# Global attention, then two local streams, against three streams in one written order (one core)

## The chip, the cores and the metric

The kernel runs on one core of one Trainium2 chip. TensorE (PE, with its weight loads as PEld), VectorE (DVE), ScalarE (ACT), GpSimd (POOL) and SyncE (SP, which issues DMAs here) each run their own list of instructions in order, and wait for one another on semaphores. The metric is the device time of one execution in microseconds, lower is better.

## The reference, cut to what matters

```python
x = L0_attn_x                                     # (8, 512, 128)
mod = (_silu(c) @ wmod).reshape(8, 6, 1, 128)     # sa, ca, ga, sb, cb, gb; |ga|, |gb| at least 0.25
h = _layernorm(x) * (1 + ca) + sa
x = x + ga * attn(h)                              # 16 heads of 8, softmax over all 512
h = _layernorm(x) * (1 + cb) + sb
x = x + gb * ffn(h)                               # two layers of the local transformer

def attn(x):          # global attention
    q, k, v = (x @ W + b).reshape(b, 16, 8, 512)
    a = softmax(einsum('bhdt,bhds->bhts', k, v) * temperature)
    return einsum('bhdt,bhts->bhds', q, a)

def layer(x, ...):    # local attention, 8 heads of 64, windows of 64
    q, k, v = split(shift_token(x) @ wqkv)
    q, k = rotary_xpos(l2norm(q) * qs, l2norm(k) * ks)
    x = x + local_attention(q, k, v) @ wo         # each window sees itself and the one before
    h = layernorm(shift_token(x)) * lg + lb
    a, g = split(h @ w1 + b1)
    return x + (a * gelu(g)) @ w2 + b2
```

All 8 batch elements ("batches" below) are independent of each other. A batch's local layers need that batch's global attention to be done.

## The kernel before

**Two phases.** The first does the global attention of all 8 batches (functions `a_...`), the second both local layers of all 8 (functions `b_...`). Every engine waits between them until the last batch of the first phase is added to `x_sb` (`a_over`).

**Phase A.** A batch takes 32 steps. In a step `a_scores` makes two 128x512 tiles of scores into one of three PSUM slots of two banks (L1072), `a_max` takes their row maxima on DVE (L828), `a_exp` makes the exponentials and their sums on ACT (L544) into `E`, a ring of four. Two steps make a group: `a_sums` inverts the sums (L832), POOL scales the queries by them (L455), and `a_values` multiplies them into `O_BANK` (L1082, 32 columns of the array for each of four heads). The scores have a contraction of 32 (four products of high and low parts by a head of 8). `k_rows` holds each head's 32 rows among 96 rows of zeros, so that one product over all 128 rows gives the head's scores; POOL zeroes it at the start (L446). Beside the steps stands the preparation of the next batch (layer norm, transpose, projections, `a_split`), at fixed steps. Batches 1 to 6 run in a register loop.

**Phase B.** Two streams, x for the even batches and y for the odd ones, four each, write their steps as generators; `merge` interleaves them by one string of x and y per engine (`ORDER`). Each stream has its own buffers and four PSUM banks, used in rotation (`b_take`). A layer is: projections by `i` (q, k, v of a quarter of the tokens, L1120), squares on ACT (L575), rotation on DVE (L859, L863) and sums of squares (L867), `b_norm` over q and k of all tokens (L872) with a Newton step (L784 to L786), the scaling on POOL (L472), transposes (L1127), then 8 heads of scores (L1136 with the mask, L1143), maxima (L884), exponentials (L603), scaling (L477), transposes (L1153) and values (L1164), then the output projection (L1174), layer norm and the gated hidden layer (L1193, L915, L1199). Exponentials and GELU need different tables of ACT.

**Ahead of phase A** DVE makes the gates of all batches as 128x2048 rows (`gates`, L752 to L759) and the rotary tables (`tables`, L766 and L770).

Of the kernel before, what the change touches and what calls it, by code (L numbers as in the profile page):

```python
# [14 lines left out]
P = 128  # L15
# [3 lines left out]
HQ = 4  # L19
# [15 lines left out]

GROUPS = [(hh, j) for hh in range(HQ) for j in range(J)]
NG = len(GROUPS)
STEPS = 2 * NG
SLOTS = 3
SLOT_USES = [len(range(k, STEPS, SLOTS)) for k in range(SLOTS)]  # L40
E_RING = 4
# [4 lines left out]
PREP = ["xT", "qT", "k", "v"]  # L46
PREP_AT = {"var": 1, "rsqrt": 2, "normal": 4, "xT": 6, "hT": 8, "qT": 9, "queries": 11, "k": 11, "v": 15}
SPLIT_AT = {"k": 13, "v": 17}


STREAMS = 2
B_BANKS = 4
# [4 lines left out]
PT_SLOTS = 4  # L57
LN_CHAIN = 2 + 3
B_CHAIN = LN_CHAIN + (2 + LN_CHAIN) * L


def bank_uses():
    out = [("x2T",)]
    for l in range(L):
        for i in range(J):
            out += [("q", l, i), ("k", l, i), ("v", l, i)]
        for i in range(J):
            out += [("qT", l, i), ("kT", l, i)]
        for n in range(NU + AV_LAG):
            if n < NU and n % 2 == 0:  # L70
                out += [("sim", l, n), ("sim", l, n + 1)]
            if 0 <= n - PT_LAG < NU:
                out.append(("pT", l, n - PT_LAG))
            if n >= AV_LAG and (n - AV_LAG) % 2:
                out.append(("av", l, (n - AV_LAG) // 2))
        out += [("wo", l), ("tok", l), ("lnT", l)]
        out += [(name, l, c) for name in ("gate", "up") for c in range(3)] + [("w2", l)]
    return out + [("yT",)]


B_USES = bank_uses()
B_USE = {s: i for i, s in enumerate(B_USES)}
B_PER = [len(range(k, len(B_USES), B_BANKS)) for k in range(B_BANKS)]

# [4 lines left out]
        "xxxxxxxxxxxxxxxxyxxyxyxxyxxyyyyxxyxxxyxyyxxxyxxxxxyxyyyxyyyyyxyxxxxxxyxyyxxxyyxxxxxyyyxyxxxyyyyyyxxy"  # L89
        "xxxxxxyxxyyyxyyyxyxxxyxyyyyyyxxxyyyxyxxxyxxyyxyyyyxyyxxxxyyxxxyyxyyyyxyyyxxxxxyyxxyxxxxyxyyxyxxxxyxy"  # L90
        "xyyyyyxyxyxxxxyxxyyyyyyyyxxyyxxyyxxxxxxyyxyyyyyyxyxxxxyyxxxyyyyxyxxxyxyxxxyxxxyyxyyyyxxyxxxxxyxyyyyy"
        "yxyxxyyxyyxxxyxyyxyxxyyyxxyxxxxyyxyyyyyxyxxxxxxyxyxyyyxyyxxxxxxyyyyxxxxyxyxyyyyxxyxxxxxyxyyyyyyxyxyx"
        "xxyxxyyxyyyyyxxxyyxyyyxxxxxyyxyyyyyyxyxxxyyxxxxyyxxyyxyxxyyxxyxxxxxyyyyyyxxyxxxxxxyxyyyyxxyyyxxyyyxx"
        "yyyyxxxxyyxyyxxxyxxyyxyyyyxyxyxyxxxxyxyyxyyyyxyyyxxxxxyyxxxxxxyyxyyxyxxxxyxyyyyyyxyxyxxyxxyyyyxxxyyy"
        "xyxxyxyxyyxxxxxyyxyyyyyyxyxxxxyyxxxyyxyyxxxxxxyyyyxxyxxyxyyyyxxyxxxxxyxyyyyyyxyxxyyyyyxyxxxyyyxxxxyx"
        "yyxxxxyxyyxyyyyyyyxyyxyyyxyxxyyxxyyxyyyxyyyyyyyyyyyy"
    ),
    "DVE": (
        "xxxxxxxxxxxxxyyyyxyxxxxxxxyyxxyxxxyyxxxxxyxyyxxxxxxyyyyyyyxxxyxxyyxxyyyxxxyyxyyyxyxxyxyyyyyxxxxxxxyy"
        "yxyyxxxxxyyyyxxyxxxyxyyyxyxxxxxyxyyxxyyyyxyxxyyxyyyyyxyyyxxxxxyxxxyxyxyyyyyyyxyxxyxxyxxxyxxyxxxyyyyy"  # L100
        "xxyxxxyxyyxyxxxxxyyyyxyxxyyyxxyyyyyxxxxyxyyyyxyxxxyxyyyyyxyyyxxxyyxxxxyxxyxxyxyxyxxxxyxyyyxyxxxxxyxx"
        "xyyyxyyxxyxyyyxyyyxxxxyyyyyxxyxxyxxyyyyyxyyyxxxyxyyxxyxxxyxxxyyyyxxyxxyxxyyyxyxxxxxyyyyyxxyyxyxxyyxy"
        "yyxxxyyxyyyxxyxxyxyyyyyxxxxyxyyxxxyyxxyyxxxyyxxyxxxyxyyyxxyxxxxyyyxxxyyyyyxxxyyxyyyyxyyyyxyxxxxxxyxx"
        "yxyyyyyyyyxyyxxyxxxxyxyyxxyxxxyyxxyxxxyxyyxyxxxxxyyyyxyxyxyyxxyyxyyyxxxyyxyyyxyxxxyxyyyyyxyyyxxxyyxx"
        "xxyyyxxyxxxyxxyxxxyxyyxyxxxxxyyyyyyyyyyyyyyyxxxyyyyxyxyyyyyyyyyy"
    ),
    "ACT": (
# [20 lines left out]
def merge(streams, order):  # L128
    for c in order:
        next(streams["xy".index(c)])  # L130
# [1210 lines left out]
```

## Time and profile before

| what | us |
|---|---|
| median of 3 runs | 1343.25 (1342.24 to 1343.5) |
| the profiled execution's own time | 1344.58 |
| its span, first to last instruction | 1342.2 |
| PE busy | 1093.8 |
| DVE busy | 978.8 |
| ACT busy | 912.8 |
| POOL busy | 466.6 |

The profiled execution lies 1.3 us over the median. No engine is busy for the whole span, so the question at every place is which engine is nearest to full there and what holds it up. Busy time of PE is modelled at its ends and its matmuls overlap, so it is read as a load with some air in it.

### The profile page before, as it was taken

What the parts mean: (1) busy time and instruction counts of PE and PEld (TensorE: products, weight loads), DVE (VectorE), ACT (ScalarE), POOL (GpSimd) and SP (SyncE); (2) the same over time, 40 slices, a digit from 0 to 9 for tenths busy, and PEclk for the clock granted to TensorE, in tenths of its full rate; (3) what the DMA queues carried; (4) which work ended last, traced back from release to release, by engine and by line L of the source; (5) the groups of instructions that cost most, each with busy time, mean ns of one, the idle gap of its engine ahead of it and who ended that gap; (6) DMA issues with size and microseconds to landing.
All of it is one profiled execution on the core that took longest, in us unless ns stands there. A gap on an engine that the chain in (4) does not pass through costs nothing. (4 is left out here: it accounts for less than half of the span.)

```text
span 1342.2 us, 24422 instructions
## 1 busy us (share of the span) xinstructions
PE 1093.8 (81%) x8120; PEld 569.9 (42%) x8120; DVE 978.8 (73%) x1937; ACT 912.8 (68%) x2746; POOL 466.6 (35%) x524
## 2 busy tenths in 40 slices
PE   4588888888888668988878789787888887888886
PEld 3233233233232235555545555454544454454553
DVE  5989888988988777668567586575775766856843
ACT  1588897898888736766646667566576574766662
POOL 2000000000000057357254464362653634545630
PEclk9699998999999979999888999888999998899988
DMA  5442241340331001110101101101001010111010
GB/s 182 161 126 64 64 126 32 94 118 25 109 103 23 0 0 30 29 29 1 37 0 37 28 2 29 36 1 36 9 21 29 1 37 0 37 29 29 1 29 16
DMA packets 24546, 59.04 MB, mean 44 GB/s; under 512 B 2736, under 2 KB 2928, under 8 KB 23280
## 3 DMA queue, kind: packets, MB, share of 16 engines
q1 hardware_dynamic: 24432, 57.62, 15.2%
q8 instruction: 59, 0.97, 0.3%
q14 instruction: 55, 0.45, 0.1%
HBM read 23.98 MB, written 18.87 MB: 32 GB/s over the span
## 5 line engine op out<-in xcount | busy, mean ns | idle before, releaser
L544 ACT ACTIVATE E<-slot,neg_max 128x512 f32<-128x512 f32 x512 | 344.2, 731 | 76.8 <-DVE neg_max L828 68.8
L828 DVE TENSOR_REDUCE neg_max<-slot 128x2 f32<-128x1024 f32 x256 | 306.0, 1212 | 39.6 <-PE slot L1072 39.5
L1072 PE MATMUL slot<-v_rows,k_rows 128*128 128x512 f32 x512 | 214.1, 489 | 61.1 <-ACT E L544 50.5
L477 POOL TENSOR_TENSOR rot_work<-rot_work,rz 128x512 f32<-128x512 f32 x128 | 133.2, 1042 | 325.0 <-DVE rz L889 324.9
L603 ACT ACTIVATE rot_work<-bank,neg 128x128 f32<-128x128 f32 x512 | 181.2, 376 | 64.6 <-DVE neg L884 41.6
L1072 PEld LDWEIGHTS slot<-v_rows,k_rows 128*128 128x128 f32 x512 | 92.1, 197 | 245.4 <-ACT E L544 213.2
L1120 PE MATMUL bank<-wqkv_sb,hs 128*128 128x512 f32 x384 | 188.2, 617 | 8.3 <-DVE rot_work L863 4.8
L463 POOL TENSOR_TENSOR work<-work,rot_work 128x512 f32<-128x512 f32 x128 | 162.9, 1273 | 78.3 <-DVE rot_work L863 74.4
L455 POOL TENSOR_TENSOR qz<-qT,rz 128x32 f32<-128x32 f32 x128 | 30.7, 240 | 416.9 <-DVE rz L832 416.9
L1082 PE MATMUL o_bank<-E,qz 128*32 128x512 f32 x1024 | 143.6, 635 | 1.7 <-POOL qz L455 1.7
L472 POOL TENSOR_TENSOR work<-work,rn 128x512 f32<-128x512 f32 x128 | 131.2, 1061 | 23.4 <-DVE rn L786 23.4
L544 ACT ACTIVATION_READ_ACCUMULATOR E<-slot,neg_max 128x1 f32 x512 | 127.5, 249 | 0.0
L884 DVE TENSOR_REDUCE neg<-bank 128x4 f32<-128x512 f32 x128 | 85.6, 679 | 45.1 <-PE bank L1143 44.7
L603 ACT ACTIVATION_READ_ACCUMULATOR rot_work<-bank,neg 128x1 f32 x512 | 109.9, 215 | 0.0
L1193 PE MATMUL bank<-work,w_sb 128*128 128x512 f32 (+1 forms) x192 | 104.4, 687 | 4.9 <-ACT work L618 2.7
L1153 PE MATMUL bank<-ident,rot_work 128*128 128x128 f32 x512 | 84.5, 292 | 25.7 <-POOL rot_work L477 13.6
L859 DVE TENSOR_TENSOR work<-bank,rot 128x512 f32<-128x512 f32 x128 | 86.7, 677 | 19.4 <-ACT rot_work L575 19.2
L575 ACT ACTIVATE rot_work<-bank 128x512 f32<-128x512 f32 x128 | 76.8, 613 | 34.9 <-PE bank L1120 20.1
L1120 PEld LDWEIGHTS bank<-wqkv_sb,hs 128*128 128x128 f32 x384 | 67.0, 193 | 75.9 <-issue 49.7
L1153 PEld LDWEIGHTS bank<-ident,rot_work 128*128 128x128 f32 x512 | 60.7, 147 | 70.7 <-POOL rot_work L477 45.2
L863 DVE TENSOR_TENSOR rot_work<-bank,rot 128x512 f32<-128x512 f32 x128 | 86.9, 679 | 0.0
L867 DVE TENSOR_REDUCE ss<-rot_work 128x8 f32<-128x512 f32 x128 | 86.3, 675 | 0.0
(120 smaller groups left out, 1652.4 us busy)
## 6 DMA issues: line engine op xcount, KB each, us to landing
v_rows<-v_scr SPq DMA_DIRECT2D x8, 1024.0 KB, 6.4
k_rows<-k_scr SPq DMA_DIRECT2D x32, 256.0 KB, 7.4
work<-v_al SPq DMA_DIRECT2D x16, 512.0 KB, 4.4
work<-v_al SPq DMA_DIRECT2D x16, 384.0 KB, 6.6
k_scr<-hi SPq DMA_DIRECT2D x16, 256.0 KB, 3.0
k_scr<-lo SPq DMA_DIRECT2D x16, 256.0 KB, 3.2
v_scr<-hi SPq DMA_DIRECT2D x16, 256.0 KB, 3.1
v_scr<-lo SPq DMA_DIRECT2D x16, 256.0 KB, 3.5
```

What stands on the lines that cost most here:

```text
L463: pool.tensor_tensor(qk[s][:, i, w, :], qk[s][:, i, w, :], sinp[s][:, n % 2, :], ALU.add).then_inc(rot_sum[s], 1)
L472: pool.tensor_tensor(v, v, rn[s][:, i, w, :].unsqueeze(2).broadcast_to([P, H, DH]), ALU.mult).then_inc(qk_ready[s], 1)
L477: pool.tensor_tensor(pr[s][:, u % PR_SLOTS], pr[s][:, u % PR_SLOTS], rz2[s][:, u, :].unsqueeze(2).broadcast_to([P, 4, 2 * W]), ALU.mult).t ...
L544: act.activation(E[:, g % E_RING, 2 * half + m, :], slot[:, m], ACT.Exp, bias=neg_max[:, n, m:m + 1], accum_out=z[:, n, m:m + 1]).then_inc ...
L603: last = act.activation(pr[s][:, u % PR_SLOTS, w, :], bank[:, 2 * W * w:2 * W * (w + 1)], ACT.Exp, bias=neg2[s][:, u, w:w + 1], accum_out= ...
L828: dve.tensor_reduce(neg_max[:, n, :], slot[:], AX.X, ALU.max, negate=True).then_inc(max_ready, 1)
L863: dve.tensor_tensor(sinp[s][:, n % 2, :].rearrange("p (h a r) -> p h a r", h=H, a=2), bank[:].rearrange("p (h a r) -> p h a r", h=H, a=2)[ ...
L1072: last = pe.matmul(bank, k_rows[:, hh, q, P * j:P * (j + 1)], v_rows[:, par, q, :], start=True, stop=True)
L1082: last = pe.matmul(O_BANK[32 * q:32 * q + 32, :], qz[:, hh, j % QZ_SLOTS, q, :], E[:, g % E_RING, q, :], start=(g == 0), stop=(g == NG - 1))
L1120: pe.matmul(bank[:], hs[s][:, P * i:P * (i + 1)], wqkv_sb[:, l, INNER * c:INNER * (c + 1)], start=True, stop=True).then_inc(full, 1)
L1153: last = pe.transpose(bank[:, P * w:P * (w + 1)], pr[s][:, u % PR_SLOTS, w, :], ident[:])
L1193: pe.matmul(bank[0:CH[c]], w1_sb[:, l, o:o + CH[c]], h2T[s], start=True, stop=True).then_inc(full, 1)
```

## The change

**Streams.** There are three generators now: `a` for global attention, `x` and `y` for the local layers. `ORDER` interleaves all three on all five engines. x takes batches 0, 1, 2, 4, 6 and begins as soon as batch 0 has left global attention; y takes 3, 5, 7 and begins when `a` is through (`enter_wait`), in the SBUF that `a` leaves. There are no register loops any more.

**Scores.** `k_rows` and `v_rows` hold 32 rows for each head, laid out so that the four heads of a group lie in different row quarters. Each score product is 32 rows by 128 columns, and the two of a step stand in neighbouring quarters. The zeroed rows and their memset are gone. Loads of `v_rows` and `k_rows` are seven DMAs each.

**Buffers.** One pool of eight PSUM banks; `BANKS` says which bank every use takes, bank 7 being `O_BANK` until `a` is over. `E` is a ring of three (four before), `kf` single (double before), `prT` two slots (four before).

**Local layers.** Projections of k and v come first, then those of q; the norm is in two halves (k, then q), each with its own `b_norm`, `b_rnorm` and pair of ACT instructions; `b_norm` takes its factor from a tensor `clamp`.

**Start.** The gates are worked out on 128x16 columns and spread by PE (16 products) and ACT (4 copies); the rotary tables are made on POOL; the first batch's `v` goes over ACT's DMA queue; the loads of `x` for batches 1 to 7 stand behind the first batch's parts.

```diff
-E_RING = 4
+E_RING = 3
...
-PT_SLOTS = 4
+PT_SLOTS = 2
...
+BATCHES = [[0, 1, 2, 4, 6], [3, 5, 7]]
+ROTATIONS = [(i, w) for w in (1, 0) for i in range(J)]
...
 ORDER = {
     "PE": (
-        "xxxxxxxxxxxxxxxxyxxyxyxxyxxyyyyxxyxxxyxyyxxxyxxxxxyxyyyxyyyyyxyxxxxxxyxyyxxxyyxxxxxyyyxyxxxyyyyyyxxy"
+        "aaaaaaaaaaaaaaaaaaaaaaaaaaaaaaaaaaaaaaaaaaaaaaaaaaaaaaaaaaxaxxxxxxxxxaaaaxxaaaaxaaaaxxxaaaaaxxxaaaaa"
...
+        def enter_wait(eng, s, k):
+            if s and k == 0:
+                a_over(eng)
...
-                for m in range(2):
-                    q = 2 * half + m
-                    bank = a_take(pe, b, n, m)
-                    last = pe.matmul(bank, k_rows[:, hh, q, P * j:P * (j + 1)], v_rows[:, par, q, :],
-                                     start=True, stop=True)
-                last.then_inc(a_full[n % SLOTS], 1)
+                pair = take_pair(pe, [("a", b, "s", n, m) for m in range(2)])
+                for m, (bank, full) in enumerate(pair):
+                    r = 32 * ((2 * half + m + hh) % HQ)
+                    pe.matmul(bank, k_rows[r:r + 32, hh, P * j:P * (j + 1)], v_rows[r:r + 32, b % 2, hh, :],
+                              start=True, stop=True).then_inc(full, 1)
...
-            pool.memset(k_rows[:].bitcast(F32), 0.0).then_inc(k_zero, 1)
+            pool.memset(qz[:], 0.0).then_inc(s_qz, 1)
+            pool.memset(clamp[:], SHIFT2).then_inc(s_clamp, 1)
...
-                dve.tensor_scalar(ss[s][:], ss[s][:], NORM_MIN2, SHIFT2, ALU.max, ALU.mult).then_inc(ss_all[s], 1)
+                v = ss[s][:, :, w, :]
+                dve.scalar_tensor_tensor(v, v, NORM_MIN2, clamp[:], ALU.max, ALU.mult).then_inc(ss_all[s], 1)
...
-            merge(streams, ORDER["DVE"])
+            merge([a_stream(), b_stream(0), b_stream(1)], ORDER["DVE"])
```

DVE at the start, before. `slot` and `gate_bc` hold the gates, `rot` the rotary tables; the last row is the first step's maxima.

```order
L822 TENSOR_TENSOR lo<-kf,hi 128x512
L752 COPY gate_bc<-slot 128x2x256 x4
L756 TENSOR_SCALAR E<-gate_bc 128x2048
L757 SCALAR_TENSOR_TENSOR E<-gate_bc 128x2048
L758 TENSOR_SCALAR E<-E 128x2048
L759 SCALAR_TENSOR_TENSOR gate_bc<-E 128x2048
L766 TENSOR_TENSOR rot<-rot,rows 128x4x64
L770 TENSOR_TENSOR rot<-rot,rows 128x4x32 x2
...
L828 TENSOR_REDUCE neg_max<-slot 128x2 x2
```

The same place now:

```order
L1131 TENSOR_TENSOR lo<-kf,hi 128x512
L1073 SCALAR_TENSOR_TENSOR gate_col<-gate_col 128x16
L1074 TENSOR_SCALAR gate_col<-gate_col 128x16
L1075 TENSOR_SCALAR gate_col<-gate_col 128x16
L1076 SCALAR_TENSOR_TENSOR gate_col<-gate_col 128x16
L1137 TENSOR_REDUCE neg_max<-psum 128x2 x2
```

Four short rows stand between the first split and the first maxima; the tables are on POOL.

DVE in global attention, before (the batch ahead of the register loop): maxima (`neg_max`), sums, and the preparation of the next batch, and nothing else.

```order
L828 TENSOR_REDUCE neg_max<-slot 128x2 x2
L832 RECIPROCAL rz<-z 128x4
L828 TENSOR_REDUCE neg_max<-slot 128x2 x2
L832 RECIPROCAL rz<-z 128x4
L815 SCALAR_TENSOR_TENSOR kf<-prep_bank,cols,rows 128x512
L820 CAST hi<-kf 128x512
```

DVE in the third batch of `a` now, with stream x's first layer (`work`, `rot_work`, `ss`, `nt`, `rn`) in between:

```order
L1210 TENSOR_REDUCE ss<-rot_work 128x8
L1216 SCALAR_TENSOR_TENSOR ss<-ss,clamp 128x4x8
L1137 TENSOR_REDUCE neg_max<-psum 128x2 x2
L1202 TENSOR_TENSOR work<-psum,rot 128x512
L1206 TENSOR_TENSOR rot_work<-psum,rot 128x512
L1210 TENSOR_REDUCE ss<-rot_work 128x8
L1141 RECIPROCAL rz<-z 128x4
L1137 TENSOR_REDUCE neg_max<-psum 128x2 x2
L1089 SCALAR_TENSOR_TENSOR nt<-ss,rn 128x4x8
```

The half norm over k stands in the middle of the rotations, and steps of `a` stand between x's.

PE in global attention, before: products of scores (`slot`) and of values (`o_bank`) by turns.

```order
L1072 MATMUL slot<-v_rows,k_rows 128x512 x4
L1082 MATMUL o_bank<-E,qz 32x512 x4
L1072 MATMUL slot<-v_rows,k_rows 128x512 x4
L1082 MATMUL o_bank<-E,qz 32x512 x4
L1072 MATMUL slot<-v_rows,k_rows 128x512 x2
```

PE where stream x begins now:

```order
L477 MATMUL psum<-ident,rot_work 128x128 x4
L429 MATMUL psum<-v_rows,k_rows 128x512 x2
L484 MATMUL psum<-wqkv_sb,hs 128x512 x9
L429 MATMUL psum<-v_rows,k_rows 128x512 x2
L405 MATMUL psum<-ident,xn 128x128 x4
L438 MATMUL psum<-E,qz 32x512 x4
L429 MATMUL psum<-v_rows,k_rows 128x512 x2
L484 MATMUL psum<-wqkv_sb,hs 128x512 x2
```

x's transposes and projections (nine in a row at one place) stand between the score products of `a`, so full-array products and 32-row products take turns.

## Rows read from the trace of the kernel before

**Rows 1.** The page's head and section 1: busy time of each engine.

```profile
span 1342.2 us, 24422 instructions
...
PE 1093.8 (81%) x8120; PEld 569.9 (42%) x8120; DVE 978.8 (73%) x1937; ACT 912.8 (68%) x2746; POOL 466.6 (35%) x524
```

**Rows 2.** Section 2 of the page: busy tenths in 40 slices.

```profile
PE   4588888888888668988878789787888887888886
...
DVE  5989888988988777668567586575775766856843
ACT  1588897898888736766646667566576574766662
```

**Rows 3.** Three lines: minimum/median/maximum ns, then first and last start, us.

```profile
L828 DVE TENSOR_REDUCE neg_max<-slot x256: 1189/1215/1226, 46.3 to 455.1; 128x2 f32<-128x1024 f32 x128
...
L840 DVE TENSOR_TENSOR x_sb<-x_sb,o_gated x8: 691/693/693, 103.9 to 460.7; 128x512 f32 x6, 128x512 f32<-128x512 f32 x2
...
L1072 PE MATMUL slot<-v_rows,k_rows x512: 387/496/796, 41.3 to 454.7; 128*128 128x512 f32 x171
```

**Rows 4.** Stretches: us, then PE, PEld, DVE, ACT, POOL busy, granted clock, DMA share, GB/s.

```profile
45.00:470.00 425.00, 357.71 (x1689) 130.62 (x1690) 368.25 (x587) 363.09 (x1056) 30.71 (x128) 0.94 0.25 76
500.00:1300.00 800.00, 671.25 (x6116) 400.83 (x6115) 542.16 (x1218) 518.20 (x1626) 404.09 (x365) 0.94 0.09 22
```

**Rows 5.** Section 5 of the page: busy us, mean ns | idle before, releaser.

```profile
L544 ACT ACTIVATE E<-slot,neg_max 128x512 f32<-128x512 f32 x512 | 344.2, 731 | 76.8 <-DVE neg_max L828 68.8
L828 DVE TENSOR_REDUCE neg_max<-slot 128x2 f32<-128x1024 f32 x256 | 306.0, 1212 | 39.6 <-PE slot L1072 39.5
L1072 PE MATMUL slot<-v_rows,k_rows 128*128 128x512 f32 x512 | 214.1, 489 | 61.1 <-ACT E L544 50.5
...
L1082 PE MATMUL o_bank<-E,qz 128*32 128x512 f32 x1024 | 143.6, 635 | 1.7 <-POOL qz L455 1.7
```

**Rows 6.** Waits in 500 to 1300 us: us in total, times, longest.

```profile
PE bank L1136 <- ACT rot_work L603: 17.5, 16, 3.6
...
PEld bank L1120 <- DVE rot_work L863: 15.9, 21, 1.6
...
PEld bank L1127 <- POOL work L472: 14.5, 24, 1.6
```

**Rows 7.** Timeline of DVE over 0 to 60 us: start us, us, instruction.

```profile
4.96 6.29 DVE L734 TENSOR_SCALAR cT<-cT 128x8 f32<-128x8 f32 x1 [0.33 <-ACT cT L516]
...
31.65 2.87 DVE L752 COPY gate_bc<-slot 128x512 f32<-128x512 f32 x4 [3.63 <-PE slot L1039]
...
46.28 2.35 DVE L828 TENSOR_REDUCE neg_max<-slot 128x2 f32<-128x1024 f32 x2
...
49.94 0.17 DVE L781 TENSOR_SCALAR var_e<-mv 128x4 f32<-128x4 f32 x1
```

**Rows 8.** Timeline of POOL over the same stretch.

```profile
4.30 6.92 POOL L446 MEMSET k_rows<- 128x8192 f32 x1
```

**Rows 9.** Timeline of PE at the start, and in three short windows of global attention.

```profile
41.34 2.90 PE L1072 MATMUL slot<-v_rows,k_rows 128*128 128x512 f32 x6 [9.73 <-issue]
...
205.27 0.63 PE L1072 MATMUL slot<-v_rows,k_rows 128*128 128x512 f32 x2
...
210.33 0.50 PE L1072 MATMUL slot<-v_rows,k_rows 128*128 128x512 f32 x1 [0.17 <-ACT E L544]
210.76 0.95 PE L1082 MATMUL o_bank<-E,qz 128*32 128x512 f32 x4
```

**Rows 10.** Section 6 of the page, a DMA issue: KB each, us to landing.

```profile
v_rows<-v_scr SPq DMA_DIRECT2D x8, 1024.0 KB, 6.4
```

**Rows 11.** DVE's groups by form, 500 to 1300 us: busy us, mean ns.

```profile
L872 DVE TENSOR_SCALAR ss<-ss 128x64 f32<-128x64 f32 x15 | 12.2, 811 | 0.4
...
L781 DVE TENSOR_SCALAR var<-mv 128x4 f32<-128x4 f32 x21 | 7.6, 362 | 0.7
...
L784 DVE SCALAR_TENSOR_TENSOR nt<-ss,rn 128x64 f32<-128x64 f32 x15 | 3.6, 237 | 1.4 <-ACT rn L585 1.2
```

More of the change, by code:

```diff
@@ L321, in b_see, with place, empty @@
-        def b_see(eng, s, k, step):
-            m, n = b_at(step)
-            eng.wait_ge(b_full[s][m], k * B_PER[m] + n + 1)
-            return banks[B_BANKS * s + m], b_free[s][m]
-        def b_done(eng, s, k, *steps):
+        bank_of = iter(BANKS)
+        places, used = {}, [0] * 8
+        def place(m, step):
+            places[step] = (m, used[m])
+            used[m] += 1
+            return psum[:, m], full[m]
+        def empty(pe, m):
+            if used[m]:
+                pe.wait_ge(free[m], used[m])
+            elif m == 7:
+                a_over(pe)
@@ new lines, in take, with take_pair, see @@
+        def take(pe, step, *read):
+            m = int(next(bank_of))
+            empty(pe, m)
+            done(pe, *read)
+            return place(m, step)
+        def take_pair(pe, steps, *read):
+            m = int(next(bank_of))
+            empty(pe, m)
+            empty(pe, m + 1)
+            done(pe, *read)
+            return place(m, steps[0]), place(m + 1, steps[1])
+        def see(eng, step):
+            m, n = places[step]
+            eng.wait_ge(full[m], n + 1)
+            return psum[:, m], free[m]
@@ L327, in b_done, with see_pair, done @@
+        def see_pair(eng, first, second):
+            m, _ = places[first]
+            see(eng, second)
+            return psum[:, m:m + 2], (free[m], free[m + 1])
+        def done(eng, *steps):
             need = {}
             for step in steps:
-                m, n = b_at(step)
+                m, n = places[step]
                 need[m] = max(need.get(m, 0), n + 1)
             for m, n in need.items():
-                passed(eng, b_free[s][m], k * B_PER[m] + n)
+                eng.wait_ge(free[m], n)
@@ L334, in stand, with b_take, b_see, b_done @@
+        def b_take(pe, s, k, step, *read):
+            return take(pe, (s, k) + step, *((s, k) + r for r in read))
+        def b_see(eng, s, k, step):
+            return see(eng, (s, k) + step)
+        def b_done(eng, s, k, *steps):
+            done(eng, *((s, k) + step for step in steps))
         def stand(eng):
@@ new lines, in gate_rows @@
+            def gate_rows():
+                pe.wait_ge(s_gcol, 1)
+                for g in range(2):
+                    for n in range(2):
+                        bank, full = take(pe, ("gate", g, n))
+                        for i in range(4):
+                            c = g * B + 4 * n + i
+                            last = pe.matmul(bank[:, D * i:D * (i + 1)], gate_col[:, 0, c:c + 1].broadcast_to([D, P]),
+                                             ident[:], start=True, stop=True)
+                        last.then_inc(full, 1)
@@ L1053, in a_project_q @@
-                pe.matmul(bank[:], wq_sb, hT[:].rearrange("p j n -> p (j n)"), start=True, stop=True).then_inc(p_full, 1)
+                bank, full = take(pe, ("a", b, "qT"), ("a", b, "xT"))
+                pe.matmul(bank, wq_sb, hT[:].rearrange("p j n -> p (j n)"), start=True, stop=True).then_inc(full, 1)
             def a_project(b, step):
                 w = wk_sb if step == "k" else wv_sb
-                bank = p_take(pe, b, step)
+                bank, full = take(pe, ("a", b, step))
```

1583 lines of the change are left out of this document (801 added, 782 removed).

## The prediction

> **What bounds the kernel now.** I read the page's head first, then the slices, then stretches, then the groups. The head says that no engine is full: PE is busy 1093.8 us of 1342.2, DVE 978.8, ACT 912.8 [rows 1]. So the order of the work costs time, and a merge can give back at most the difference between 1342 and about 1094. The slices show two regimes [rows 2]: up to slice 13 all three engines stand at 8 or 9, afterwards PE stands at 7 to 9 and DVE and ACT at 5 to 7.
>
> The border is in the source rows: global attention runs from the first maxima at 46.3 us to the last residual, which ends at 461.4 [rows 3]. That is 415.1 us, 51.9 for a batch. The local layers take the 880.8 us that are left, 110.1 for a batch with two streams side by side.
>
> The stretches give the loads [rows 4]. In global attention, over 425 us: DVE 368.25, ACT 363.09, PE 357.71, so 46.0, 45.4 and 44.7 us per batch; the fullest engine, DVE, reaches 0.866. POOL is nearly idle there (30.71). In the local layers, over 800 us (7.27 batches at 110.1): PE 671.25, DVE 542.16, ACT 518.20, POOL 404.09, so 92.4, 74.6, 71.3 and 55.6 us per batch; the fullest, PE, reaches 0.839. Global attention is thus bound by DVE and ACT, the local layers by PE, and the two are never beside each other: the change puts them there.
>
> **The score products.** Today 512 products occupy PE for 214.1 us, 0.42 each [rows 5]. Two of them back to back cover 0.63 us [rows 9], and the shortest record of one is 387 ns [rows 3], so the pitch is about 0.24. The values' products show what quarters of the array do: 1024 of 635 ns, a sum of 650 us, in 143.6 us of busy time [rows 5]; four run at once, since 4 of them cover 0.95 us [rows 9]. If row quarters do the same, a pair takes one pitch fewer. The saving lies between 0 and 214.1/2 = 107 us of PE time, 0 to 13.4 per batch. I take 10, since the pairs also have latency that stays. PE was not the fullest engine in that phase, so alone this gives no time; it makes room for stream x: PE 34.7 per batch of `a`.
>
> Against that stands the change of the array's form. Inside one form the pitch is 0.24, and from a score product at 210.33 to the values' at 210.76 it is 0.43 [rows 9], up to 0.2 us for one change of form. Stream x's full-array products now come between 32-row products, so I add one or two changes to each of some 220 steps: 220 x 0.1 to 220 x 0.4, 22 to 88 us of PE; I take 40. The Trainium skill (TensorEngine Tiling (Array Packing), Key Properties) says the same, that changing the tiling mode drains the engine while changing only the tile does not; it gives no figure. By that rule the larger end would hold, PE would have 48 us more than I take, and the sum below would grow only if PE became the bound.
>
> **The start.** Today the first score product runs at 41.34 after 9.73 us of idle PE [rows 9], which is the wait for the loads of `v_rows` and `k_rows` (`v_rows` needs 6.4 us to landing [rows 10]); the first maxima come only at 46.28, because gates and tables hold DVE from 31.65 [rows 7]. The change takes those 14.6 us off DVE; by themselves they hide the loads, so just 46.28 - 41.34 = 4.9 us of them count. DVE's first small instruction also took 6.29 us, and it ended as POOL's memset of `k_rows` ended, at 11.2 [rows 7, 8]; others of its size take 0.2. Without that memset the chain may start up to 6 us earlier. The Trainium skill (SBUF — State Buffer, SBUF: two separate sides) describes DVE and GpSimd sharing a port pair under an exclusive lock, which is what these two rows look like. Against it: 14 loads instead of 5 behind one another, some of 3 us of issue, and ACT issues `v`'s DMAs in front of its gate copies and first exponentials. So the first maxima come at 35 to 44; I take 38.
>
> **Phase 1, `a` beside x.** The order table says how far things get. x's first step on DVE stands behind 1.12 batches of `a`, and ahead of the last step of `a` stand 204 steps of x of 87 per batch, 2.34 batches (PE's table gives 2.32). The first 1.13 batches run as today: 1.13 x 51.9 = 59 us. It remains 6.87 batches of `a` and 2.33 of x:
> DVE: 6.87 x 46.0 + 2.33 x 75 = 491; ACT: 6.87 x 45.4 + 2.33 x 72 = 480 (0.7 a batch for its new pair of instructions in each layer); PE: 6.87 x 34.7 + 2.33 x 92.4 + 40 = 494; POOL 26 + 130 = 156.
> The norm in halves costs DVE a second clamp and three more Newton instructions: 3 x 0.24 = 0.7 us a layer; `b_norm` itself, 811 ns for 64 columns, is dear today [rows 11] and may cost 0.3 to 0.8 each. That is -0.2 to +1.5 us a layer, and I have put 0.4 a batch. POOL beside `a` also hurts DVE's short instructions: L781 takes 362 ns in the local layers [rows 11] and 0.17 us where POOL is idle [rows 7]. About 13 such a batch at half of 0.19, since POOL is half as busy here, are 8 us in all. DVE: 499.
> What share of the time can it be busy? 0.866 was reached with one stream, 0.839 by PE with two. Here three engines are near equal, which leaves no slack, but each wait of `a` can now be filled by x. Lower bound 0.80, upper 0.95; I take 0.89, a little over `a` alone: 499/0.89 = 561. Phase 1 ends at 38 + 59 + 561 = 658.
>
> What is queued behind the new waits: `a_exp` of group g now waits for the values of group g-3 (a ring of three), and those wait on PE for POOL's scaling, in front of which x's 1.0 to 1.3 us steps stand in POOL's list. While PE waits there, x's products wait too. I count nothing for it beyond the 0.89, since the sums are ready about two steps ahead.
>
> **Phase 2, x beside y.** It remains 8 - 2.33 = 5.67 batches; at today's pace 5.67 x 110.1 = 624 us. About 8 us of that go, since today both streams enter empty (slice 14 shows PE at 6 [rows 2]) and now x is in the middle of a layer. The pool of banks and the early k half can take away at most the waits of PE for banks and for POOL's scaled tiles: (15.9 + 17.5 + 14.5)/7.27 = 6.6 us a batch [rows 6], 37 us in all; the two slots of `prT` work against it, since the ACT copy of the next pair now waits for the values of the last one. From -10 to 37; I take 16. Phase 2: 600 us.
>
> **Sum.** 658 + 600 = 1258, and 2.4 us outside the span (1344.58 - 1342.2): 1260 us, 6.2% below the median. Of the 83 us, phase 1 carries all: 2.33 batches of local layers have cost 257 us and now cost 658 - 461 = 197.
>
> **Rivals.**
> 1. *Near-full merge.* DVE at 0.95 in phase 1 (525 us), first maxima at 35, and phase 2 takes the bank waits and more (575): 35 + 59 + 525 + 575 + 2 = 1196. For it: two independent streams seldom wait at once, and the whole order is written out. Against: neither phase of before came over 0.87. Chance 0.15.
> 2. *y's chain paces phase 2.* y must do three batches after `a`. A stream of before needs 880.8/4 = 220 us a batch; 3 x 220 = 660 instead of 600, so 1320. For it: steps within a layer depend on each other, and y cannot start earlier. Against: the tables let y go ahead (x has done 2.6 of its last batches when y is at 2.9). Partly so: 1280 to 1320. Chance 0.17.
> 3. *Row quarters don't overlap, and forms drain dearly.* PE in phase 1 then has 494 + 69 + 48 = 611, and at 0.93 it needs 657 instead of 561: 1356 at the worst, about 1300 if only one of the two holds. Against: the column quarters overlap fully [rows 5, 9]. Chance 0.08.
> 4. *Slower.* The ring of three and POOL's order stop PE, and PE's list stops x as well. DVE's share in phase 1 decides: with phase 2 at 624, the total reaches 1343 when the stretch takes 620 us, a share of 0.80. On a share of 0.84, 20 of the 110 groups held up 1.3 us each are enough for that; at 0.76 the time is 1380. Today such waits of PE are 1.7 us in all [rows 5], with POOL idle. Chance 0.06.
> That `a` and x don't in fact overlap is no rival here: the order rows show them interleaved.
>
> **Chances and range.** The forecast (1225 to 1280) has 0.54. The range 1195 to 1330 takes in the near-full merge and y's chain, and leaves out rival 4, the worst of 3 and what lies below 1195, together under 0.2. A difference of 0.2% is about what a measurement of this kernel can tell from no change. Faster by more: 0.93; within: 0.01; slower: 0.06.
>
> **What would show it.** First maxima at 38 (35 to 44). The last residual of `a` at 658; DVE's share between x's start and there 0.89. Score products in pairs, both starting within some 20 ns, with a total busy time near half of 214 us. Phase 2 of 600 us with PE at 0.87 or more. If PE waits for `qz` for more than 20 us in phase 1, rival 4 is at work; if PE stands under 0.8 in phase 2 while y never waits for x, rival 2. The forecast is wrong in its core if phase 1 takes over 740 us or DVE's share there is under 0.8.

## The result and the profile after

| | before | after |
|---|---|---|
| median, us | 1343.38 (1342.24 to 1346.27) | 1305.48 (1304.58 to 1308.16) |
| span of the profiled execution, us | 1342.2 [rows 1] | 1303.6 |
| granted clock, mean | 0.935 | 0.895 |
| end of global attention, us | 461.4 [rows 3] | 707.3 |

The ratio is 0.9718, with a 95% interval of 0.9697 to 0.9739: 37.9 us less. The forecast was 1260, 83 us less. The direction was right and the time lies inside the range, but under half of the gain arrived. In the experiments below a ratio leaves out executions that took over 1.5% longer than the fastest of the same kernel.

The page of after, its head, three of its slice lines and four groups (columns as in [rows 1, 2, 5]):

```profile
span 1303.6 us, 23771 instructions
...
PE 1065.7 (82%) x8124; PEld 530.6 (41%) x8124; DVE 976.1 (75%) x1985; ACT 923.0 (71%) x2782; POOL 466.8 (36%) x537
...
PE   4078878988878789878888889898888988888987
...
DVE  3096988897788789787996875876795688677755
...
PEclk8575889988888999698788999989999989999999
...
L843 ACT ACTIVATE E<-psum,neg_max 128x512 f32<-128x512 f32 x512 | 348.3, 714 | 100.0 <-DVE neg_max L1137 77.5
L1137 DVE TENSOR_REDUCE neg_max<-psum 128x2 f32<-128x1024 f32 x256 | 306.9, 1213 | 86.4 <-PE psum L429 85.3
...
L429 PE MATMUL psum<-v_rows,k_rows 32*128 32x512 f32 x512 | 137.2, 556 | 99.6 <-ACT E L843 45.8
```

The slices show two things. The second one, 33 to 65 us, is all but empty: PE, which began with 4 and 5 before [rows 2], has 4 and 0. And from there PE stands mostly at 8 and 9, in the first half together with DVE. The idle time of DVE before its maxima has grown from 39.6 us [rows 5] to 86.4; one wait at the start makes 42.7 us of it.

The phases are read off three lines of after: the score maxima, the last residual of global attention, and `kT`'s memset, the first instruction on DVE that belongs to one local stream alone (first x, then y). Minimum/median/maximum ns, then first and last start:

```profile
L1137 DVE TENSOR_REDUCE neg_max<-psum x256: 1153/1216/1226, 63.5 to 693.9; 128x2 f32<-128x1024 f32 x128
...
L1152 DVE TENSOR_TENSOR x_sb<-x_sb,kf x8: 691/692/1040, 128.5 to 706.6; 128x512 f32<-128x512 f32 x8
...
L1279 DVE MEMSET kT<- x2: 272/272/272, 129.2 to 709.0; 128x256 f32 x2
```

| term | forecast | after | error |
|---|---|---|---|
| first maxima | 38 | 63.5 | +25.5 |
| `a` alone, 1.13 batches | 59 | 65.7 | +6.7 |
| `a` beside x | 561 | 578.1 | +17.1 |
| x beside y | 600 | 596.3 | -3.7 |
| span | 1258 | 1303.6 | +45.6 |

More than half of the error is there before the first maximum is taken. The timeline of after, PE and then ACT's and SP's queues (start us, us, instruction, idle before it; ACTq and SPq issue DMAs):

```profile
20.79 6.10 PE L397 MATMUL psum<-ident,gate_col 128*128 128x128 f32 x32 [4.38 <-DVE gate_col L1076]
62.60 1.22 PE L429 MATMUL psum<-v_rows,k_rows 32*128 32x512 f32 x6 [35.71 <-DMA v_rows<-v_scr]
...
26.93 13.64 ACTq L857 DMA_DIRECT2D v_rows<-v_scr  x7
...
24.81 7.41 SPq L655 DMA_DIRECT2D k_rows<-k_scr  x7
32.27 14.26 SPq L639 DMA_DIRECT2D x_sb<-in_x  x7
```

PE had done everything else by 26.9 us and stood 35.71 us for `v_rows`. Before, PE was idle for 9.73 us at this place [rows 9; the row names no releaser], and the megabyte needed 6.4 us to landing [rows 10]. Now the issue alone takes 13.64 us, and the last part lands at about 62.

Three stretches of after (us, then PE, PEld, DVE, ACT, POOL busy with counts, granted clock, DMA share, GB/s): `a` alone, `a` beside x, x beside y:

```profile
63.50:128.00 64.50, 50.36 (x222) 14.83 (x220) 50.90 (x87) 50.59 (x147) 4.09 (x17) 0.63 0.21 70
128.00:707.00 579.00, 484.58 (x3333) 204.74 (x3333) 485.84 (x888) 473.79 (x1422) 157.54 (x229) 0.89 0.17 54
707.00:1300.00 593.00, 515.40 (x4508) 297.88 (x4503) 428.36 (x975) 392.83 (x1206) 294.80 (x267) 0.95 0.08 21
```

The middle one is the merge: DVE 0.839, PE 0.837, ACT 0.818 of the time. The last has PE at 0.869, against 0.839 in the local layers before [rows 4]. The clock is new: 0.63 while `a` runs alone, where global attention had 0.94 before [rows 4].

### The profile page after: what moved, and what is told of

Read it like the earlier page. It is cut to its first block and busy times, and to the rows that moved or that the text cites. A ratio compares the mean times of both kernels' runs of the same rounds, so it can differ in the third digit from the quotient of the medians.

```text
span 1303.6 us, 23771 instructions
## 1 busy us (share of the span) xinstructions
PE 1065.7 (82%) x8124; PEld 530.6 (41%) x8124; DVE 976.1 (75%) x1985; ACT 923.0 (71%) x2782; POOL 466.8 (36%) x537
## 5 line engine op out<-in xcount | busy, mean ns | idle before, releaser
L843 ACT ACTIVATE E<-psum,neg_max 128x512 f32<-128x512 f32 x512 | 348.3, 714 | 100.0 <-DVE neg_max L1137 77.5
L1137 DVE TENSOR_REDUCE neg_max<-psum 128x2 f32<-128x1024 f32 x256 | 306.9, 1213 | 86.4 <-PE psum L429 85.3
L429 PE MATMUL psum<-v_rows,k_rows 32*128 32x512 f32 x512 | 137.2, 556 | 99.6 <-ACT E L843 45.8
L484 PE MATMUL psum<-wqkv_sb,hs 128*128 128x512 f32 x384 | 195.7, 636 | 11.5 <-DVE rot_work L1206 3.8
L939 ACT ACTIVATE rot_work<-psum,neg 128x128 f32<-128x128 f32 x512 | 184.3, 407 | 26.4 <-DVE neg L1228 18.5
L438 PE MATMUL psum<-E,qz 128*32 128x512 f32 x1024 | 164.2, 718 | 0.0
L939 ACT ACTIVATION_READ_ACCUMULATOR rot_work<-psum,neg 128x1 f32 x512 | 124.8, 247 | 0.0
L843 ACT ACTIVATION_READ_ACCUMULATOR E<-psum,neg_max 128x1 f32 x512 | 118.6, 232 | 0.0
L491 PE MATMUL psum<-ident,work 128*128 128x128 f32 x512 | 89.2, 312 | 29.4 <-POOL work L784 14.0
L559 PE MATMUL psum<-work,w_sb 128*128 128x512 f32 (+1 forms) x192 | 99.4, 645 | 6.7 <-ACT work L954 4.3
```

The source lines that it names most:

```text
L429: pe.matmul(bank, k_rows[r:r + 32, hh, P * j:P * (j + 1)], v_rows[r:r + 32, b % 2, hh, :], start=True, stop=True).then_inc(full, 1)
L438: last = pe.matmul(O_BANK[32 * q:32 * q + 32, :], qz[:, hh, j % QZ_SLOTS, q, :], E[:, (b * NG + g) % E_RING, q, :], start=(g == 0), stop=( ...
L484: pe.matmul(bank, hs[s][:, P * i:P * (i + 1)], wqkv_sb[:, l, INNER * c:INNER * (c + 1)], start=True, stop=True).then_inc(full, 1)
L491: last = pe.transpose(bank[:, P * p:P * (p + 1)], qk[s][:, i, w, P * p:P * (p + 1)], ident[:])
L559: pe.matmul(bank[0:CH[c]], w1_sb[:, l, o:o + CH[c]], h2T[s], start=True, stop=True).then_inc(full, 1)
L843: act.activation(E[:, (b * NG + g) % E_RING, 2 * half + m, :], pair[:, m], ACT.Exp, bias=neg_max[:, n, m:m + 1], accum_out=z[:, n, m:m + 1 ...
```

## Experiments

The ratios below are to the kernel before, run on the same chip; its medians there lie between 1343.2 and 1346.8.

### One DMA for each head's 32 rows

**Theory A**: the new loads are slow because of their shape. The view of the source for two to four heads is `"q t d s -> q (t d) s"`, with the heads outermost, a dimension of 2, 3 or 4, where before it was 128 rows for `v_rows` (`"q h t d s -> (h t d) q s"`) and 32 for each part of `k_rows`. **Theory B**: the number of DMAs and their issue are the cost; more of them are slower still. The edit gives each head its own DMA (16 instead of 7 for each of `k_rows` and `v_rows`), whose outermost dimension is the 32 rows.

```diff
-K_LOADS = [1, 2, 2, 2]
+K_LOADS = [4, 4, 4, 4]
...
-                for q in ((0, HQ),) if hh == 0 else ((0, HQ - hh), (HQ - hh, HQ)):
-                    r = 32 * ((q[0] + hh) % HQ)
-                    sp.dma_start(dst[r:r + 32 * (q[1] - q[0])].bitcast(F32),
-                                 scr[q[0]:q[1], hh].rearrange("q t d s -> q (t d) s")).then_inc(landed, 16)
+                for q in range(HQ):
+                    r = 32 * ((q + hh) % HQ)
+                    sp.dma_start(dst[r:r + 32].bitcast(F32),
+                                 scr[q, hh].rearrange("t d s -> (t d) s")).then_inc(landed, 16)
```

> The changed kernel with each load of k_rows and v_rows cut into single heads of 32 rows (64 KB), 16 DMAs instead of 7, the same bytes to the same places. Theory A (shape of the loads): a DMA whose outermost dimension on the DRAM side counts 2, 3 or 4 heads is moved by only 2, 3 or 4 of the 16 DMA engines, and that is what holds the first score product until 62.6 us; with 32 rows outermost all 16 work, v_rows lands some 7 us after its last issue, the first maxima come at 38 to 43 instead of 63.5, and the 4.9 us wait at the first border of batches goes too: 1305.5 - 25 = about 1280, 1276 to 1286. Theory B (volume or queue): the loads are slow because the x and weight loads run beside them, or because ACT's queue is slow; more and smaller DMAs then change nothing or cost issue time: 1303 to 1312 and first maxima at 60 or later.

Measured: 1268.31 us (1262.82 to 1270.2), ratio 0.9425 (0.9379 to 0.9471). Its span was 1266.2, 37.4 less than after's. PE and the queues at its start:

```profile
39.38 1.22 PE L429 MATMUL psum<-v_rows,k_rows 32*128 32x512 f32 x6 [12.58 <-DMA v_rows<-v_scr]
...
26.85 7.50 ACTq L857 DMA_DIRECT2D v_rows<-v_scr  x16
...
25.03 7.45 SPq L655 DMA_DIRECT2D k_rows<-k_scr  x16
32.52 3.46 SPq L639 DMA_DIRECT2D x_sb<-in_x  x7
```

Sixteen DMAs take 7.50 us to issue where seven took 13.64 (on SP, `k_rows` takes 7.45 where it took 7.41), and the wait falls from 35.71 to 12.58 us. So Theory A, with 12 us more of gain than it had expected; the next experiment looks for them. How many engines move the data is shown by the DMA view over the stretch in which `v_rows` is on its way, first after from 29 to 62 us, then this kernel from 26 to 40 (busy tenths of the core's 16 DMA engines in 40 slices; then ACT's queue, q10, with packets, MB and share of 16 engines):

```profile
DMA  2523222211669841297886897899998999994111
...
q10 hardware_dynamic: 557, 1.05, 9.6%
```

```profile
DMA  6548587838886999997999977899999969999999
...
q10 hardware_dynamic: 793, 1.08, 30.2%
```

The same megabyte is spread over 33 us at 9.6% of 16 engines (16 x 0.096, one and a half at work), or goes through in 14 us at 30.2% (nearly five, with the keys' loads and weights on the rest). The Trainium skill (DMA: Bandwidth & Descriptors, Why a DMA increments its semaphore by 16 and not by 1) has the rule: a DMA runs on as many engines, 16 at most, as divide the slowest dimension of both sides. By it a source with 2, 3 or 4 heads outermost gets at most that many and one with 32 rows gets 16. Both traces agree with that, though they show shares of a stretch and not the engines of one DMA. This edit changes the number of DMAs together with their shape; that the number isn't what helps is seen in the kernel before, where a single DMA with 128 rows outermost brought the same megabyte in 6.4 us [rows 10].

### The loads of the first batch alone

Is it the start alone, or every border of batches? Only batch 0's loads are split by head; the later ones keep their shape.

```diff
+                if first:
+                    for q in range(HQ):
+                        ...
+                    return
...
-                a_rows(k_rows[:, hh], k_scr, hh, k_in[hh])
+                a_rows(k_rows[:, hh], k_scr, hh, k_in[hh], b == 0)
```

> The changed kernel with per-head loads for the first batch alone; the loads of the seven batches after it keep the changed kernel's shape. It splits the 37 us that per-head loads gave (1305.5 to 1268.3). Theory A: the first batch's loads, which nothing hides, are 23 us of it (first maxima at 40.2 instead of 63.5), and the later loads the other 14, by waits at the batches' borders and by SP's queue: 1282, 1278 to 1286, and the 4.9 us wait for k_rows at the first border comes back. Theory B: the later loads are hidden, and the 14 us came from elsewhere (order of arrival after an earlier start): 1268 to 1273.

Measured: 1279.36 us (1276.66 to 1280.72), ratio 0.9508 (0.9461 to 0.9555). The maxima start at 40.3, as with all loads split (40.2), but `a` ends later. `kT`'s memset, that is x's start and y's, in this kernel:

```profile
L1293 DVE MEMSET kT<- x2: 272/272/272, 105.7 to 684.8; 128x256 f32 x2
```

With all loads split the two stand at 101.0 and 671.5: x starts 4.7 us later here, and the stretch from there to y takes 579.1 us instead of 570.5. So Theory A: about 26 us of the 37 belong to the first batch's loads and about 11 to the later ones, though those have a whole batch of time to land. In after the only visible trace of them is a wait of 4.9 us for `k_rows` at the first border; the rest I have not placed.

### What 32-row products do by themselves

**Theory A**: the new form of the product is good for the first phase or neutral, since PE isn't its fullest engine. **Theory B**: it has a price of its own, which the merge hides. The kernel before, with products over the 32 rows in which a head's data stand (same values, same order; both products of a step in one row quarter):

```diff
+                    r = slice(32 * hh, 32 * hh + 32)
-                    last = pe.matmul(bank, k_rows[:, hh, q, P * j:P * (j + 1)], v_rows[:, par, q, :],
+                    last = pe.matmul(bank, k_rows[r, hh, q, P * j:P * (j + 1)], v_rows[r, par, q, :],
```

> The kernel before with only the form of the score products changed: 32 rows (the head's own) instead of 128 rows of which 96 are zeros. Both products of a step lie in the same row quarter, so they can't run at once; layout, loads and order are as before. Theory A (32-row products lower the granted clock): in global attention the clock falls from 0.95 to 0.8 or less, as in the changed kernel's first batch (0.63), and a batch takes 54 to 57 us instead of 51.9: 1343 + 16 to 40 = 1360 to 1383. Theory B (the clock was low in the changed kernel only because PE had stood idle for 36 us and x had not begun): the clock stays at 0.93 to 0.95 and the time within 4 us of 1343.

Measured: 1454.72 us (1451.42 to 1459.26), ratio 1.0823 (1.0772 to 1.0874): 110 us slower through this edit alone. Global attention, and the local layers behind it:

```profile
45.00:575.00 530.00, 512.54 (x1684) 179.01 (x1684) 365.42 (x562) 368.43 (x1052) 30.79 (x128) 0.55 0.20 61
600.00:1400.00 800.00, 662.84 (x6052) 397.05 (x6052) 550.20 (x1235) 515.32 (x1606) 410.43 (x372) 0.94 0.09 22
```

To be set beside [rows 4]: DVE and ACT have the same work (365.42 and 368.43 us against 368.25 and 363.09), PE has 512.54 instead of 357.71 with the same count, and the granted clock is 0.55 instead of 0.94, that is, the array was at the lower of its two levels (1.2 GHz) for most of the phase. The local layers are untouched. PE had become the bound. Is the reason its clock, or the form itself, with its changes between score and value products? Three stretches of this phase in the same trace, at three mean clocks, answer (the first two are short, half a batch each):

```profile
120.00:145.00 25.00, 22.36 (x110) 8.79 (x106) 21.53 (x31) 20.12 (x57) 1.68 (x7) 0.86 0.16 47
195.00:220.00 25.00, 23.42 (x105) 8.72 (x107) 20.62 (x30) 20.55 (x61) 1.69 (x7) 0.77 0.56 158
245.00:570.00 325.00, 321.14 (x1006) 112.40 (x1006) 213.02 (x311) 219.45 (x624) 18.28 (x76) 0.50 0.17 52
```

At a clock of 0.86 DVE is busy for 0.861 of the time (21.53 of 25), as in the kernel before (0.866); at 0.77 for 0.825; at 0.50, the lower level throughout, for 0.655. PE runs 3.1 products per us there, against 4.4 in the first stretch. So most of the loss goes with the clock; why the clock stays low is not shown. The loss was far more than either expectation held.

### One after the other

Does the merge pay, then? Loads split by head, and the order table of the three streams rewritten, and with it the bank table `BANKS`: first all of `a`, then x's part of 2.33 batches alone, then x beside y as in after.

```diff
 ORDER = {
     "PE": (
-        "aaaa...aaxaxxxxxxxxxaaaaxxaaaaxaaaa..."
+        "aaaa...aaaaaaaaaaaa...xxxxxxxxxxxx..."
```

> Per-head loads, and the order tables changed so that all of a's steps come first and then x's steps that stood between them (2.33 batches); what follows is the same. Nothing overlaps in phase 1. It shows what a costs alone in its new form and what x costs alone. Theory A (phase 1 is short of engine time, DVE above all): a alone takes 52 to 56 us a batch, 415 to 450 in all, x alone 2.33 batches of 150 to 190 us (it is bound by the chain of its own steps), 350 to 440; phase 1 then takes 770 to 890 and the run 1400 to 1530. Theory B (a in its new form is itself slow, which eats the overlap): a alone takes over 480 us.

Measured: 1573.05 us in one run, span 1571.2. `a` alone and x alone:

```profile
41.00:563.00 522.00, 392.35 (x1690) 111.14 (x1684) 367.53 (x562) 369.67 (x1052) 30.56 (x128) 0.63 0.21 63
600.00:900.00 300.00, 193.77 (x1499) 115.55 (x1500) 121.57 (x271) 124.58 (x394) 87.70 (x80) 0.77 0.06 14
```

`a` needs 521.5 us, over the 480 of Theory B, and x's part 416 (562.8 to 978.9), 938 together; merged, with the same instructions and loads, they take 630 (40.2 to 669.8). Both sides run badly alone: `a` at a clock of 0.63 and no engine over 0.76, x at 179 us for a batch and no engine over 0.65. Beside each other they have a clock of 0.91 and three engines at 0.83 to 0.85. So the merge is worth 308 us against its own parts run one by one. Against the kernel before the same work is 42 us shorter (415 for global attention and 2.33 x 110.1 = 257 for local layers make 672), since there `a` alone took 51.9 us a batch and not 65.2, and the local layers ran two side by side. The 65.2 are not the clock's alone: between 60 and 560 us PE waited 113.8 us for exponentials, and ACT 59.9 us for value products, whose end frees a place in the ring of three; and in the run with split loads the first 1.13 batches, at the same clock of 0.63, took 60.8 us, 53.8 a batch. How the 13.3 us a batch divide is open.

### Does the low clock of `a` alone cost time in the new kernel?

**Theory A**: yes, the first 1.13 batches would be shorter at full clock. **Theory B**: no. On top of split loads, one unused product over all rows stands ahead of each pair of score products, in batch 0 and six steps of batch 1 (its result is overwritten).

```diff
+                if b == 0 or (b == 1 and n < 6):
+                    pe.matmul(pair[0][0], k_rows[:, hh, P * j:P * (j + 1)], v_rows[:, b % 2, hh, :],
+                              start=True, stop=True)
```

> Per-head loads, and in the first batch of a (and 6 steps of the second), where x hasn't begun, one full-array product of 128 rows per step into the bank that the step's real product then overwrites; its result is not used. Theory A (32-row products alone don't keep the clock up, and the low clock costs time there): the granted clock between 40 and 101 us rises from 0.63 to 0.9 or more, the first batch takes 52 to 54 us instead of 60.8 for 1.13, that is 5 to 8 us less: 1260 to 1264. Theory B (the clock is low for the idle PE ahead of it, or costs nothing there): no change, 1266 to 1271.

Measured: 1273.11 us (1268.65 to 1277.31), ratio 0.9463 (0.9407 to 0.9518). From 40 to 106 us, split loads first, then with the product added:

```profile
40.00:106.00 66.00, 53.90 (x237) 15.71 (x231) 56.61 (x110) 53.52 (x156) 4.06 (x17) 0.63 0.36 119
```

```profile
40.00:106.00 66.00, 60.66 (x270) 21.74 (x274) 53.56 (x94) 51.73 (x150) 4.06 (x17) 0.84 0.37 123
```

The clock rises from 0.63 to 0.84, as Theory A had it, and the batch is no shorter, as Theory B had it (62.3 us from the first maxima to x's start, against 60.8): PE's busy time rises from 53.90 to 60.66 us, so the added products eat what the clock gives. No time is to be had in this way; that a full clock for nothing would save none is not shown.

The same product in every step of `a`:

> Per-head loads, and the unused 128-row product in every step of a. It adds 256 products, at 0.23 to 0.43 us each 59 to 110 us of PE work, and raises the clock of phase 1 beyond its 0.91. Theory A (PE has room in phase 1 and the clock is what it lacks): 1250 to 1264. Theory B (PE's time in phase 1 is as short as DVE's; x's own full-array products keep the clock up already): the added work costs 10 to 50 us, 1278 to 1318.

Measured: 1302.78 us (1298.09 to 1308.47; a fourth execution took 1325.6), ratio 0.9707 (0.964 to 0.9774), which is Theory B's. The whole merge, from x's start to y's, here and then with split loads alone:

```profile
104.70:705.40 600.70, 543.27 (x3568) 237.34 (x3566) 488.95 (x891) 477.45 (x1425) 157.45 (x229) 0.94 0.18 52
```

```profile
101.00:671.50 570.50, 477.22 (x3348) 204.07 (x3348) 485.35 (x891) 473.02 (x1423) 157.31 (x229) 0.91 0.19 54
```

The 220 added products bring 66 us of PE time, at a clock of 0.94 instead of 0.91, and the merge is 30 us longer: about half of what is added comes through. PE is busy for 0.90 of the time here and DVE for 0.81, where both stood at 0.84 to 0.85. So PE's time is short in the merge too, though PE can be filled to 0.90 there.

And in the kernel before with 32-row products (the product on top of that edit):

> The kernel before with 32-row products (as in the run that took 1454.7 us) and one unused 128-row product per step in front of them. Theory A (the 111 us came from the granted clock, 0.55 in global attention, and not from the 32-row form's own duration or from changing forms): the clock goes back to 0.9 or more and global attention to 415 to 440 us although PE has 256 products more: 1343 to 1368. Theory B (32-row products are slow by themselves): 1455 or more, since work is only added.

Measured: 1554.57 us (1505.74 to 1570.28). Its executions lie too far apart for a ratio; the spread goes with the clock (0.808 at 1570, 0.850 at 1506). All four are above the 1454.72 without the product. The profiled one is among the longest (1570.12), so its rows are read against each other alone. Two stretches of it:

```profile
45.00:200.00 155.00, 155.00 (x394) 55.24 (x393) 80.32 (x127) 79.20 (x220) 5.97 (x25) 0.50 0.19 61
200.00:400.00 200.00, 195.14 (x763) 70.78 (x763) 144.14 (x225) 143.27 (x407) 11.95 (x50) 0.84 0.22 65
```

In the first PE is busy without a gap and stays at the lower level; in the second the clock is there, and DVE's work per us rises by 39% (144.14/200 against 80.32/155). Theory B's number held (1455 or more), but not its reason, since the pace follows the clock. Theory A's reason fits, but its remedy failed: full-array products between the 32-row ones don't bring the clock back reliably. What decides is open.

### The ring of three for E

Rival 4 rested on it. On split loads, `E_RING = 4`:

> Per-head loads and E as a ring of four instead of three. Theory A (the short ring stops ACT's exponentials, and with them PE and x): phase 1 is 10 to 25 us shorter than with per-head loads alone. Theory B (the ring matters little: the exponentials waited for the value products 10.0 us in all between 70 and 700 us): 0 to 8 us shorter.

Measured: 1268.31 us (1264.71 to 1272.68), ratio 0.9424 (0.9383 to 0.9465), no difference. In this order of steps the ring of three costs nothing that can be measured.

### What is late next at the start

On split loads `v_rows` gets a counter for each group, so that the first product waits for the first 4 of its 16 loads only; beside it, the kernel with split loads once more.

```diff
-                if n == 0:
-                    passed(pe, v_in, (b + 1) * 16 * V_LOADS)
                 if n % (STEPS // HQ) == 0:
+                    passed(pe, v_in[hh], (b + 1) * 16 * HQ)
```

> Per-head loads, and the landing of v_rows counted by one semaphore for each group of heads, so that the first score product waits for 4 of the 16 loads of v and not for all. With one semaphore PE stood idle 12.6 us ahead of its first product at 39.4, until the last load of v. Theory A (the last loads of v hold the start): the first maxima come at 34 to 37 instead of 40.2, and the time falls by 3 to 6 us against per-head loads alone. Theory B (k_rows or the parts are just behind, or the later groups' loads stop PE a little further on): 0 to 2 us.

> The kernel with per-head loads a second time, on the same chip as the one with a semaphore per group, so that the two can be set against each other: 1265 to 1272.

Measured: 1270.4 us (1268.87 to 1275.0) and 1268.19 (1264.55 to 1274.15), ratios 0.9442 (0.9402 to 0.9481) and 0.9419 (0.9377 to 0.9461). The maxima start at 31.8 us instead of 41.6, and x starts at 100.5 instead of 102.4: the ten microseconds are given back within a batch, and the time is the same (Theory B). The waits of DVE from 25 to 60 us (us in total, times, longest) and the row behind the second of them say where:

```profile
DVE neg_max L1137 <- PE psum L428: 13.9, 3, 11.4
DVE stats L1080 <- DMA x_sb<-in_x: 7.9, 1, 7.9
```

```profile
42.00 0.87 DVE L1080 BATCH_NORM_STATS2 stats<-x_sb 128x6 f32<-128x128 f32 x4 [7.89 <-DMA x_sb<-in_x]
```

DVE takes two maxima, then stands at the norm of batch 1, whose `x` is the first of seven loads behind the keys on SP, and it waits for all seven. So batch 1's `x` goes ahead of the first parts, with a counter of its own:

```diff
+            a_load(1, x_second)
             a_parts(0, 0)
...
-            for b in range(1, B):
+            for b in range(2, B):
...
+                elif b == 1:
+                    dve.wait_ge(x_second, 16)
```

> Loads head by head, a counter for each group's v_rows, and now the load of batch 1's x ahead of the first parts' stores, with a counter of its own (before, DVE waited for all seven x loads together). Where only the counters were split, the first maxima came at 31.8 us instead of 41.6, and the time stayed, since DVE then stood 7.89 us at the norm of batch 1 until the x loads had landed (42.0 us). Theory A, this wait is the next late link of the start: it goes, x's start comes 5 to 9 us earlier than at 100.5 us, and the span is 1258 to 1263. Theory B, the batch is held by something else too (the step's pace at the lower granted clock, x's start by its own preparation): x's start stays within 2 us of 100.5 and the span at 1265 to 1271.

> The kernel with loads head by head and split counters once more, beside the one with the early load of batch 1's x: 1268 to 1272, both theories.

Measured: 1263.2 us (1256.32 to 1272.55), ratio 0.9381 (0.9345 to 0.9417), and 1273.97 (1265.62 to 1280.98), ratio 0.9476 (0.9439 to 0.9513) without the early load. No wait of DVE for `x_sb` is left, and x starts at 92.3 us, against 101.9 without the early load:

```profile
L1282 DVE MEMSET kT<- x2: 272/272/272, 92.3 to 674.5; 128x256 f32 x2
```

Theory A: x's start is 8 to 10 us earlier. Of the six spans (1254.5 to 1270.7) the profiled one is the longest; in it the merge took longer (y at 674.5) with a clock of 0.89. So the gain of this step rests on six executions a side, whose intervals don't touch (0.9417 and 0.9439), and not on the profiled one. It is the lowest median of the study: 6.2% under before, some 42 us under the changed kernel. The same kernel without the early load gave 1270.4 and 1273.97 in two rounds, so single microseconds between rounds mean nothing, and against the first run with split loads (0.9379 to 0.9471) the intervals overlap.

## Why the prediction was right in direction and wrong in size

**The start: the step that failed.** I priced the loads as "14 loads instead of 5 behind one another, some of 3 us of issue" and took 38 us for the first maxima, 35 to 44 as bounds. I counted the DMAs and took their size per microsecond from [rows 10], where the outermost dimension was long, without looking at what the new view has outermost. The maxima came at 63.5. With nothing but the shape put right the first maxima came at 40.2, inside my 35 to 44. (The "3 us of issue" stands in no row of before's start either: there SP issued all four loads of `k_rows` in 2.42 us.) The earlier start came as forecast: `v_rows` was first issued at 26.93 us instead of 33.59. That the memset of `k_rows` had held DVE fits: its first small instruction, which took 6.29 us [rows 7], is now this (timeline of DVE in after), though no run took the memset away by itself, and none put the gates or tables back:

```profile
4.65 0.69 DVE L1054 TENSOR_SCALAR cT<-cT 128x8 f32<-128x8 f32 x1 [4.65 <-ACT cT L817]
```

So the step that failed is the price of the first batch's loads, 25.5 us too low. The later loads, which have no term in my sum, took about 11 more.

**`a` alone.** 59 forecast, 65.7 in after, 60.8 with the loads right, the latter at a clock of 0.63.

**`a` beside x.** 561 forecast, 578.1, and 568.8 with the loads right. Two misses cancel in part, which is luck: with the loads right DVE's load was 484 us, not 499, and its share 0.85, not 0.89. For the share, the run with a product added in every step shows that PE's time was short as well: half of what was added came through. I had named three near-equal engines as a reason against, and still went above the share of `a` alone. Why DVE's load is smaller I haven't split up. Rival 1, a merge with DVE at 0.95, did not happen.

**Score products.** Rival 3 is refuted. Two rows of PE's timeline of after in the merge show a pair in 0.50 us, about the 0.497 of one product (median 496 in [rows 3]), where two took 0.63 [rows 9]:

```profile
205.27 0.50 PE L429 MATMUL psum<-v_rows,k_rows 32*128 32x512 f32 x2 [0.71 <-ACT E L843]
205.70 1.06 PE L438 MATMUL psum<-E,qz 128*32 128x512 f32 x8
```

Their busy time fell from 214.1 to 137.2 us, 77 of the 107 that I gave as the bound; I took 80. But the value products beside them, 143.6 us before [rows 5], now need 164.2, so PE gained 56 us in the two together (group of after, 63 to 707 us):

```profile
L438 PE MATMUL psum<-E,qz 128*32 128x512 f32 x1024 | 164.2, 718 | 0.0
```

PE's load in the merge was 484.6 against my 494, so the 40 us for changes of form were not too small as a sum; they were not measured by themselves. What I didn't see is the clock. In the kernel before, 32-row products alone lengthen global attention from 415 to 530 us, most of it with the clock. In the new kernel `a` alone ran at 0.63, and the clock of 0.89 came only in the merge, in which x's full-array products run beside it. The working used [rows 4]'s loads, measured at 0.94, for a form that runs otherwise.

**x beside y.** 600 forecast, 596.3. PE at 0.869, the 0.87 that I named. The 16 us that I took for banks and the early k half, and the 8 for the full start, were not tested one by one. Rival 2, y's chain as the pace, did not happen.

**Rival 4.** PE's waits for `qz` make 1.3 us in after, and the ring of four changed nothing.

**The sum.** With the loads' shape put right: 40.2 + 60.8 + 568.8 + 596.4 = 1266.2, against 1258. So of 45.6 us of error 37.4 are the shape of a DMA and 8 all else. One sentence of the prediction doesn't follow from its own terms: "Of the 83 us, phase 1 carries all". Its 257 against 197 are 60 us, and the other 24 are phase 2's 624 against 600. Measured in the same way, after has 11 in phase 1 (257 against 245.9) and 28 in phase 2 (624 against 596.3); with the loads right they are 49 and 28. So phase 2 gave what was forecast, and all that was missing is phase 1's.

## What to carry to other kernels

When a layout changes, look at the outermost dimension on both sides of every DMA that moves it, before its bytes and its count: here sixteen DMAs with 32 rows outermost beat seven with up to 4 heads outermost. Phases bound by different engines are worth merging, and the load of the fullest engine over a share taken from the phases before foretold the merged one within 3%, with two misses that partly cancel (0.85 was measured where I took 0.89). A change of a product's form must be priced with the clock it gets, not only with its count and pitch; and after an early wait is removed, the next late load is sought before the gain is counted.

## What the runs showed of the hardware

**PE's busy share alone does not tell the clock.** In the kernel before with 32-row products PE is busy 512.5 of 530 us at a granted clock of 0.55, and 321.1 of the 325 us from 245 to 570 at 0.50; in the kernel before it is busy 357.7 of 425 us at 0.94 [rows 4]. The Trainium skill (TensorE: Matmul & The Clock Gate, Part 1: The HAM clock gate) says that the gate is set by how busy the PE has been recently; by that the first two would have had the full clock. The measurement decides. The only edit between these kernels is the 32 rows of the score products; by what way it lowers the clock is not settled.

**On ACT's queue seven DMAs of up to four heads each took 13.64 us to issue, sixteen of one head 7.50.** The seven loads of `x`, which are the same in both kernels and stand behind `k_rows` on SP, went from 14.26 to 3.46 us in the same way. That loads behind a slow transfer are issued more slowly too was not in my sum.
